# A gated normalisation kernel on one core: the last product of a set's factor moves from DVE to POOL, and a set's chain gets a fourth step

## The chip, the core and the metric

The kernel runs on one core of one Trainium2 chip. The metric is the device time of one execution in microseconds (us). A core has five engines that run side by side, each through its own list of instructions in order: TensorE (PE, matrix products; its weight loads are shown apart as PEld), VectorE (DVE), ScalarE (ACT), GpSimd (POOL) and SyncE (SP, which here only starts loads from memory). They meet through semaphores: an instruction raises one when it is done, and another engine waits until it has reached a count.

## What is computed

x has the shape 8 x 128 x 256 x 256 in float32: 8 batches, 128 channels, 65,536 pixels.

```
def _gn(v, G=32, eps=1e-5):          # per batch, 32 groups of 4 channels
    m, s = mean and variance of a group over its channels and all pixels
    return ((v - m) / sqrt(s + eps))
def _L0_conv_ref(v, W, b):           # v = _gn(x)
    u, var = mean and variance (ddof=1) of v over the 128 channels, per pixel
    n_x = (v - u) / (sqrt(var) + 1e-6)
    n_x = einsum('bchw,oc->bohw', n_x, W) + b
    return v * n_x
out = x + _L0_conv_ref(_gn(x), W, b)
```

So the statistics of a whole batch have to be known before its first pixel can be normalised, and every pixel then needs the reciprocal of its own deviation over the channels. That reciprocal is called the factor.

## The kernel before, in words

**Slots, steps and sets.** A batch is cut in 64 slots of 1,024 pixels (128 partitions by 1,024 columns, 512 KB). One step of the main loop takes one slot through each stage, every stage behind the other by a fixed lag. Four slots make a set, and the small operations on variance and factor are done once for a set, on tiles of 128 by 128. I call a step by its number modulo 4 its phase, 0 to 3.

**What a step does.** POOL normalises the next step's slot in place (L447, `norm`). ACT squares the slot of this step (L575). PE sums slot and squares over the channels (L737), into the set's sums in `sums_ps`. Seven steps behind, PE spreads the factor of a slot to all partitions (L723, into `factor_ps`). Eight steps behind, DVE multiplies the slot by it (L648, `scale`) and PE projects it with W (L749, 16 matrix instructions). Nine steps behind, DVE forms the gated product in place (L662, `gate`), and POOL adds the mean back (L458, `finish`). Ten steps behind, ACT issues the store (L603). PE's order in a step is spread, project, sums. PE's spread waits until DVE's `scale` of the slot before has read `factor_ps`, and DVE's `gate` waits for the projection of its slot.

**A set's chain of small operations.** Counted from the set's first step, it was:

- lag 4, phase 0: ACT squares the channel sums (L594), DVE forms the variance (L668, L672);
- lag 5, phase 1: ACT takes the root, the root plus epsilon and the root squared (L580 to L584), DVE the reciprocal (L680, `approx`), POOL a subtraction and two products that correct it (L491, L465, L467, tile `root`);
- lag 6, phase 2: DVE subtracts 2 from the correction and multiplies by `approx` (L684), which is the factor. Then it is split in three bfloat16 pieces, so that PE can spread it: ACT takes a first piece (L587), POOL the rest (L472), ACT a second piece (L590), POOL the last (L477, `pieces`);
- lag 7, phase 3: PE spreads it.

In ACT's list a pass over a slot of the next batch's statistics stands between the two pieces.

**The next batch's statistics.** While a batch is computed, the 64 slots of the next one are read for mean and variance: 24 by DVE, two `bn_stats` each (L693, L694), at steps of phase 3, two slots at nine of these steps and one at five of them (11, 23, 35, 47 and 55); 40 by ACT, two passes each (L515), in steps 1 to 57. In a step of phase 0, ACT's order is: squares, one pass, the square of the channel sums (L594), the other passes. At steps 58 to 62 the group statistics are worked out by a chain over DVE, ACT and PE.

**Buffers and loads.** x is held in 50 buffers of one slot. 34 slots of the 64 (`KEPT`) stay in their buffer from the statistics to the output; the other 30 are loaded again (`streamed`, L410). The loads for the statistics are L413: item i of 30 to 63 brings the i-30th kept slot. A planner (`Places`) gives each load a planned step: `STATS_LEAD` or `LEAD` steps ahead of its use or earlier, so that two loads are `LOAD_GAP` apart. The plan sets only their order and their buffers. SP goes through that order and issues a load as soon as its buffer is free, which for a kept slot is when that slot's store of the batch before it in the buffer has landed; all later loads wait behind it.

Of the kernel before, what the change touches and what calls it, by code (L numbers as in the profile page):

```python
# [28 lines left out]
KEPT_UNTIL = 42  # L29
# [5 lines left out]
CHAIN_STEPS = 3  # L35

LAG_VAR = SPLIT
LAG_ROOT, LAG_FIT = LAG_VAR + 1, LAG_VAR + 2
# [7 lines left out]
STATS_LEAD = 2  # L46
STORE_STEPS = 2
DROP_STEPS = 2
LOAD_GAP = 0.64
# [140 lines left out]
def norm_gate_kernel(nc, x, w, bias, const, pick, ident, out):  # L190
# [23 lines left out]
    with ExitStack() as ctx:  # L214
# [33 lines left out]
        factor = sum_sq  # L248
# [53 lines left out]
        miss_squared = sem("miss_squared")  # L302
        factor_done = sem("factor_done")
# [128 lines left out]
        def _(pool):  # L432
# [28 lines left out]
            def correct(done):  # L461

                pool.wait_ge(approx_done, done)
                pool.wait_ge(miss_done, done)
                nc.gpsimd.tensor_tensor(miss[:, :], miss[:, :], approx[:, :], ALU.mult).then_inc(miss_scaled, 1)  # L465
                pool.wait_ge(miss_scaled, done)
                nc.gpsimd.tensor_tensor(miss[:, :], miss[:, :], approx[:, :], ALU.mult).then_inc(miss_squared, 1)  # L467

# [11 lines left out]
            def period(b, own, before, nxt):  # L480
                for step in steps(own, before, nxt):
                    root_of = set_behind(step, LAG_ROOT, b, own, before)
# [125 lines left out]
        def _(dve):  # L608
# [28 lines left out]
            def period(b, own, before, nxt):  # L637
                of = plan if own else first_plan
                for step in steps(own, before, nxt):
# [25 lines left out]
                    def var_of_sums(ready):  # L665

                        dve.wait_ge(sum_sq_done, ready)
                        nc.vector.scalar_tensor_tensor(out=var_ps(step - LAG_VAR), in0=sum_sq[:, :], scalar=-1.0 / P,  # L668
                                                       in1=sums_of(step - LAG_VAR)[:, 1, :], op0=ALU.mult, op1=ALU.add)\
                            .then_inc(var_sum_done, 1)  # L670
                        dve.wait_ge(var_sum_done, ready)
                        nc.vector.tensor_scalar(var[:, :], var_ps(step - LAG_VAR), TINY, 1.0 / (P - 1), ALU.max, ALU.mult)\  # L672
                            .then_inc(var_done, 1)
# [4 lines left out]
                    if (ready := set_behind(step, LAG_ROOT, b, own, before)) is not None:  # L678
                        dve.wait_ge(root_eps_done, ready)
                        nc.vector.reciprocal(approx[:, :], approx[:, :]).then_inc(approx_done, 1)  # L680
                    if (ready := set_behind(step, LAG_FIT, b, own, before)) is not None:

                        dve.wait_ge(miss_squared, ready)
                        nc.vector.scalar_tensor_tensor(out=factor[:, :], in0=miss[:, :], scalar=-2.0, in1=approx[:, :],  # L684
                                                       op0=ALU.add, op1=ALU.mult).then_inc(factor_done, 1)
# [110 lines left out]
```

## Time and profile before

| | us |
|---|---|
| time, median of 3 runs | 1874.69 (1874.65 to 1875.2) |
| the profiled execution: its own time | 1875.25 |
| its span from first to last instruction | 1873.4 |
| PE busy | 1695.9 (91%) |
| DVE busy | 1695.0 (90%) |
| ACT busy | 1481.7 (79%) |
| POOL busy | 1455.2 (78%) |

The granted TensorE clock was 0.997 of full speed. 394.49 MB were read and 268.44 MB written, 354 GB/s over the span. Busy time is the union of an engine's instructions; how long an engine waited, and for whom, is in other views, which are shown in the section of rows below.

### The profile page before, as it was taken

How to read it: one execution, taken by the hardware profiler on the slowest of the kernel's cores; microseconds unless marked ns; L12 is line 12 of the kernel's file. 1: busy time of each engine (PE TensorE's matmuls, PEld its weight loads, DVE VectorE, ACT ScalarE, POOL GpSimd, SP SyncE). 2: the span in 40 equal slices, each digit the busy share in tenths (PEclk: the TensorE clock that was granted, in tenths of full speed). 3: DMA queues.
4: the chain of work that ended last, by engine and by line, in shares of the span. 5: the costliest groups of instructions: out<-in, count | busy, mean ns of one | idle time of the engine just before them, and what ended most of it. 6: DMA issues, size and time to landing. Idle time of an engine off the chain costs nothing.

```text
span 1873.4 us, 67650 instructions
## 1 busy us (share of the span) xinstructions
PE 1695.9 (91%) x28706; PEld 918.7 (49%) x28706; DVE 1695.0 (90%) x2000; ACT 1481.7 (79%) x2634; POOL 1455.2 (78%) x1684
## 2 busy tenths in 40 slices
PE   0069999999999999999999999999999999999998
PEld 0045555555555555555555555555555555555553
DVE  5659998999989998999989999999999999888887
ACT  5689887888878887898878889788887988744442
POOL 0058888887888888788788788887887888888885
PEclk9999999999999999999999999999999999999999
DMA  9979999999999999999999999999999999854775
GB/s 375 409 271 370 379 382 329 400 390 397 367 326 413 387 390 349 361 416 378 390 329 395 402 384 379 336 402 389 391 357 356 416 379 398 301 209 188 272 269 216
DMA packets 183037, 667.33 MB, mean 356 GB/s; under 512 B 20560, under 2 KB 20944, under 8 KB 182736
## 3 DMA queue, kind: packets, MB, share of 16 engines
q1 hardware_dynamic: 109008, 394.54, 56.8%
q10 hardware_dynamic: 73728, 268.47, 35.9%
q8 instruction: 227, 3.72, 0.7%
q14 instruction: 74, 0.61, 0.1%
HBM read 394.49 MB, written 268.44 MB: 354 GB/s over the span
## 4 chain that ended last, share of the span: by engine, by line
PE 66%; DVE 15%; issue 6%; DMA 6%; POOL 3%; ACT 2%; SPq 2%; POOLq 0%; ACTq 0%; DVEq 0%
PE proj_ps L749 39%; PE sums_ps L737 15%; PE factor_ps L723 12%; DVE scaled L648 5%; DVE bn L693 4%; DVE bn L694 4%; DMA tiles<-x 4%; SPq L413 2%; DMA out<-tiles 2%; DVE tiles L662 1%; POOL tiles L458 1%; POOL tiles L447 1%; ACT unused L515 1%; ACT squares L575 0%; POOL pieces L477 0%
## 5 line engine op out<-in xcount | busy, mean ns | idle before, releaser
L749 PE MATMUL proj_ps<-scaled,w_t 128*32 128x512 f32 x8192 | 984.9, 598 | 0.1
L458 POOL TENSOR_SCALAR tiles<-tiles,columns_sb 128x1024 f32<-128x1024 f32 x512 | 575.0, 1123 | 231.4 <-DVE tiles L662 227.9
L662 DVE SCALAR_TENSOR_TENSOR tiles<-proj_ps,columns_sb,tiles 128x1024 f32<-128x1024 f32 x512 | 643.6, 1257 | 73.2 <-PE proj_ps L749 71.8
L515 ACT ACTIVATE unused<-tiles,bn 128x1024 uint8<-128x1024 f32 x560 | 635.1, 1134 | 0.0
L648 DVE TENSOR_TENSOR scaled<-tiles,factor_ps 128x1024 f32<-128x1024 f32 x512 | 619.1, 1209 | 10.7 <-PE factor_ps L723 6.5
L447 POOL TENSOR_SCALAR tiles<-tiles,columns_sb 128x1024 f32<-128x1024 f32 x512 | 617.1, 1206 | 13.8 <-DMA tiles<-x 12.8
L575 ACT ACTIVATE squares<-tiles 128x1024 f32<-128x1024 f32 x512 | 537.7, 1050 | 66.1 <-PE sums_ps L737 30.7
L737 PEld LDWEIGHTS sums_ps<-tiles,const_sb 128*32 128x32 f32 x8192 | 245.2, 111 | 317.1 <-issue 263.0
L749 PEld LDWEIGHTS proj_ps<-scaled,w_t 128*32 128x32 f32 x8192 | 213.5, 109 | 360.7 <-issue 306.6
L723 PE MATMUL factor_ps<-pieces,pick_sb 128*128 128x128 bf16 x4096 | 317.7, 220 | 63.3 <-DVE scaled L648 48.4
L737 PE MATMUL sums_ps<-tiles,const_sb 128*32 128x128 f32 x8192 | 319.8, 274 | 13.4 <-ACT squares L575 13.4
L737 PE MATMUL sums_ps<-squares,const_sb 128*32 128x128 f32 x8192 | 319.0, 274 | 0.0
L723 PEld LDWEIGHTS factor_ps<-pieces,pick_sb 128*128 128x128 bf16 x4096 | 231.5, 98 | 172.0 <-issue 76.7
L737 PEld LDWEIGHTS sums_ps<-squares,const_sb 128*32 128x32 f32 x8192 | 235.5, 111 | 0.2
L587 ACT ACTIVATE piece<-sum_sq,const_sb 128x128 bf16<-128x128 f32 x128 | 51.4, 402 | 118.7 <-DVE sum_sq L684 117.5
L680 DVE RECIPROCAL approx<-approx 128x128 f32<-128x128 f32 x128 | 121.3, 948 | 9.9 <-ACT approx L582 7.8
L693 DVE BATCH_NORM_STATS2 bn<-tiles 128x6 f32<-128x512 f32 x168 | 114.4, 681 | 0.0
L694 DVE BATCH_NORM_STATS2 bn<-tiles 128x6 f32<-128x512 f32 x168 | 113.6, 676 | 0.0
L515 ACT ACTIVATION_READ_ACCUMULATOR unused<-tiles,bn 128x1 f32 x560 | 104.9, 187 | 0.0
L760 PE MATMUL sums_ps<-gn,const_sb 128*128 128x1 f32 x16 | 3.2, 271 | 87.7 <-ACT gn L539 87.7
L590 ACT ACTIVATE piece<-sum_sq,const_sb 128x128 bf16<-128x128 f32 x128 | 51.5, 402 | 34.8 <-POOL sum_sq L472 34.8
L441 POOL COPY columns_sb<-new_scalars 128x2 f32<-128x2 f32 x8 | 1.5, 185 | 99.4 <-ACT new_scalars L562 99.4
(58 smaller groups left out, 769.6 us busy)
## 6 DMA issues: line engine op xcount, KB each, us to landing
tiles<-x SPq DMA_DIRECT2D x752, 512.0 KB, 8.5
out<-tiles ACTq DMA_DIRECT2D x512, 512.0 KB, 7.1
const_sb<-const SPq DMA_DIRECT2D x1, 86.0 KB, 1.9
scaled<-w SPq DMA_DIRECT2D x1, 64.0 KB, 2.1
scaled<-ident SPq DMA_DIRECT2D x1, 64.0 KB, 2.0
pick_sb<-pick SPq DMA_DIRECT2D x1, 8.0 KB, 1.8
columns_sb<-bias SPq DMA_DIRECT2D x1, 0.5 KB, 2.4
```

Source lines behind the costliest of these rows:

```text
L447: nc.gpsimd.tensor_scalar(place(s), place(s), norm_scalars[:, 0:1], norm_scalars[:, 1:2], ALU.add, ALU.mult).then_inc(normed, 1)
L458: nc.gpsimd.tensor_scalar(place(s), place(s), 1.0, out_shift[:, 0:1], ALU.mult, ALU.add).then_inc(finished, 1)
L515: nc.scalar.activation(unused[:, which, :], data, (ACT.Identity, ACT.Square)[which], bias=pivot_of(of), scale=-1.0, accum_out=act_sums[:, ...
L575: nc.scalar.activation(squares[:, step % 2, :], place(step), ACT.Square).then_inc(squared, 1)
L648: nc.vector.tensor_tensor(scaled[:, s % 2, :], place(s), factor_ps[:, :], ALU.mult)\
L662: nc.vector.scalar_tensor_tensor(out=place(s), in0=proj_ps[:, s % 2, :], scalar=gate_shift[:, 0:1], in1=place(s), op0=ALU.add, op1=ALU.mul ...
L680: nc.vector.reciprocal(approx[:, :], approx[:, :]).then_inc(approx_done, 1)
L693: nc.vector.bn_stats(bn_of(of)[:, j, :], data[:, 0:BANK])
L694: nc.vector.bn_stats(bn_of(of)[:, j + 1, :], data[:, BANK:SLOT]).then_inc(bn_done, 1)
L723: mm = nc.tensor.matmul(factor_ps[:, chunk(h, t)], pick_sb[:, j:j + 1].to_broadcast([P, P]), pieces[:, s // SPLIT % 2, :], start=True, sto ...
L737: mm = nc.tensor.matmul(sums_of(s)[32 * t:32 * t + 32, which, :], rows, data[:, chunk(h, t)], start=(which == 0 and k == 0), stop=(which = ...
L749: mm = nc.tensor.matmul(proj_ps[q:q + 32, s % 2, h:h + BANK], w_t[:, q:q + 32], scaled[:, s % 2, h:h + BANK], start=True, stop=True)
```

## The change

The product that ends the factor is taken off DVE. POOL does it in two instructions, a shift by -2 and a product, right behind its two correcting products. DVE's reciprocal and POOL's operations move from lag 5 to lag 6 (`LAG_INVERSE`), the pieces from lag 6 to lag 7, and with the longer chain every later stage (spread, scale, gate, store) by one step. The factor is now written into `var` in place of `sum_sq`, so DVE's write of `var` waits for the pieces of the set before. The last kept slot moves from 40 to 42, loads for statistics are planned 1 step ahead of use (it was 2) and at 0.6 steps from each other (it was 0.64). The number of kept slots and so of loads stays.

```diff
-KEPT_UNTIL = 42
+KEPT_UNTIL = 44
...
-CHAIN_STEPS = 3
+CHAIN_STEPS = 4
...
-LAG_ROOT, LAG_FIT = LAG_VAR + 1, LAG_VAR + 2
+LAG_ROOT, LAG_INVERSE, LAG_FIT = LAG_VAR + 1, LAG_VAR + 2, LAG_VAR + 3
...
-STATS_LEAD = 2
+STATS_LEAD = 1
...
-LOAD_GAP = 0.64
+LOAD_GAP = 0.6
...
-        factor = sum_sq
+        factor = var
...
                 nc.gpsimd.tensor_tensor(miss[:, :], miss[:, :], approx[:, :], ALU.mult).then_inc(miss_squared, 1)
+                pool.wait_ge(miss_squared, done)
+                nc.gpsimd.tensor_scalar(miss[:, :], miss[:, :], 1.0, -2.0, ALU.mult, ALU.add).then_inc(miss_shifted, 1)
+                pool.wait_ge(miss_shifted, done)
+                nc.gpsimd.tensor_tensor(factor[:, :], miss[:, :], approx[:, :], ALU.mult).then_inc(factor_done, 1)
...
-                    root_of = set_behind(step, LAG_ROOT, b, own, before)
+                    root_of = set_behind(step, LAG_INVERSE, b, own, before)
...
                         dve.wait_ge(var_sum_done, ready)
+                        if ready > 1:
+                            dve.wait_ge(pieces_done, ready - 1)
...
-                    if (ready := set_behind(step, LAG_ROOT, b, own, before)) is not None:
+                    if (ready := set_behind(step, LAG_INVERSE, b, own, before)) is not None:
                         dve.wait_ge(root_eps_done, ready)
                         nc.vector.reciprocal(approx[:, :], approx[:, :]).then_inc(approx_done, 1)
-                    if (ready := set_behind(step, LAG_FIT, b, own, before)) is not None:
-
-                        dve.wait_ge(miss_squared, ready)
-                        nc.vector.scalar_tensor_tensor(out=factor[:, :], in0=miss[:, :], scalar=-2.0, in1=approx[:, :],
-                                                       op0=ALU.add, op1=ALU.mult).then_inc(factor_done, 1)
```

POOL's list in the middle of a batch, from the `norm` ahead of a set's correcting operations to its last piece. Before:

```order
501 L447 TENSOR_SCALAR tiles<-tiles,columns_sb 128x1024
502 L491 TENSOR_TENSOR root<-var,root 128x128
503 L465 TENSOR_TENSOR root<-root,approx 128x128
504 L467 TENSOR_TENSOR root<-root,approx 128x128
505 L458 TENSOR_SCALAR tiles<-tiles,columns_sb 128x1024
506 L447 TENSOR_SCALAR tiles<-tiles,columns_sb 128x1024
507 L472 TENSOR_TENSOR sum_sq<-sum_sq,piece 128x128
508 L458 TENSOR_SCALAR tiles<-tiles,columns_sb 128x1024
509 L477 TENSOR_TENSOR pieces<-sum_sq,piece 128x128
```

The same stretch in the changed kernel, whose lines are numbered a little higher (L448 is `norm`, L459 `finish`):

```order
562 L448 TENSOR_SCALAR tiles<-tiles,columns_sb 128x1024
563 L496 TENSOR_TENSOR root<-var,root 128x128
564 L466 TENSOR_TENSOR root<-root,approx 128x128
565 L468 TENSOR_TENSOR root<-root,approx 128x128
566 L470 TENSOR_SCALAR root<-root 128x128
567 L472 TENSOR_TENSOR var<-root,approx 128x128
568 L459 TENSOR_SCALAR tiles<-tiles,columns_sb 128x1024
569 L448 TENSOR_SCALAR tiles<-tiles,columns_sb 128x1024
570 L477 TENSOR_TENSOR var<-var,piece 128x128
571 L459 TENSOR_SCALAR tiles<-tiles,columns_sb 128x1024
572 L482 TENSOR_TENSOR pieces<-var,piece 128x128
```

Two instructions have come in ahead of the first `finish`; the rest keeps its order, but the group of five stands in phase 2 now and the pieces in phase 3.

ACT's list at steps 22 to 24 of the first batch, where step 24 is of phase 0 and squares the channel sums of the next set. Before (L587 and L590 are the two pieces, L515 the statistics, L594 the square of the sums):

```order
109 L587 ACTIVATE piece<-sum_sq,const_sb 128x128
110 L515 ACTIVATE unused,act_sums<-tiles,bn 128x1024
111 L590 ACTIVATE piece<-sum_sq,const_sb 128x128
112 L603 DMA out<-tiles 128x1024
113 L575 ACTIVATE squares<-tiles 128x1024
114 L515 ACTIVATE unused,act_sums<-tiles,bn 128x1024 x2
115 L603 DMA out<-tiles 128x1024
116 L575 ACTIVATE squares<-tiles 128x1024
117 L515 ACTIVATE unused,act_sums<-tiles,bn 128x1024
118 L594 ACTIVATE sum_sq<-sums_ps 128x128
```

Steps 23 and 24 in the changed kernel (L592 and L595 are the pieces, L520 the statistics, L599 the square of the sums):

```order
109 L580 ACTIVATE squares<-tiles 128x1024
110 L592 ACTIVATE piece<-var,const_sb 128x128
111 L520 ACTIVATE unused,act_sums<-tiles,bn 128x1024
112 L595 ACTIVATE piece<-var,const_sb 128x128
113 L520 ACTIVATE unused,act_sums<-tiles,bn 128x1024
114 L608 DMA out<-tiles 128x1024
115 L580 ACTIVATE squares<-tiles 128x1024
116 L520 ACTIVATE unused,act_sums<-tiles,bn 128x1024
117 L599 ACTIVATE sum_sq<-sums_ps 128x128
```

Between the second piece and the square of the sums stood a store, a whole step and the beginning of the next (two squares, three passes); now one pass, a store, one squares and one pass stand there.

The third place is the end of SP's list for a batch. It reads alike but for what the buffers' last stores are: items 62 and 63 of the statistics waited for the stores of slots 39 and 40, which ACT issued in steps 49 and 50; now for those of slots 41 and 42, issued in steps 52 and 53. They are used in steps 55 and 56 in both kernels.

## Rows read from the trace of the kernel before

**Rows 1.** The page, busy time of each engine.

```profile
PE 1695.9 (91%) x28706; PEld 918.7 (49%) x28706; DVE 1695.0 (90%) x2000; ACT 1481.7 (79%) x2634; POOL 1455.2 (78%) x1684
```

**Rows 2.** Windows: busy us PE, PEld, DVE, ACT, POOL; clock, DMA share, GB/s.

```profile
580.00:600.00 20.00, 19.24 (x336) 10.56 (x332) 19.26 (x23) 17.21 (x32) 16.81 (x21) 1.00 1.03 416
...
517.00:951.00 434.00, 414.95 (x7044) 224.52 (x7036) 408.86 (x483) 374.51 (x671) 357.96 (x413) 1.00 0.99 379
```

**Rows 3.** Timeline of PE, steps 43 and 44: start, us, instruction, wait.

```profile
904.51 0.62 PE L723 MATMUL factor_ps<-pieces,pick_sb 128*128 128x128 bf16 x8
905.07 1.92 PE L749 MATMUL proj_ps<-scaled,w_t 128*32 128x512 f32 x16
...
908.62 0.62 PE L723 MATMUL factor_ps<-pieces,pick_sb 128*128 128x128 bf16 x8 [0.76 <-DVE scaled L648]
```

**Rows 4.** Timeline of DVE, steps 43 and 44, phases 3 and 0.

```profile
902.16 1.21 DVE L648 TENSOR_TENSOR scaled<-tiles,factor_ps 128x1024 f32<-128x1024 f32 x1
903.78 1.28 DVE L662 SCALAR_TENSOR_TENSOR tiles<-proj_ps,columns_sb,tiles 128x1024 f32<-128x1024 f32 x1 [0.41 <-PE proj_ps L749]
904.98 0.69 DVE L693 BATCH_NORM_STATS2 bn<-tiles 128x6 f32<-128x512 f32 x1
...
907.36 1.21 DVE L648 TENSOR_TENSOR scaled<-tiles,factor_ps 128x1024 f32<-128x1024 f32 x1
```

**Rows 5.** Waits of PE from 517 to 951 us: total, times, longest.

```profile
PE factor_ps L723 <- DVE scaled L648: 13.6, 18, 0.8
PE factor_ps L723 <- POOL pieces L477: 5.2, 4, 1.5
```

**Rows 6.** The removed product: its group, and one at 970 us.

```profile
L684 DVE SCALAR_TENSOR_TENSOR sum_sq<-root,approx 128x128 f32<-128x128 f32 x128 | 57.9, 453 | 2.6 <-POOL root L467 2.6
...
970.74 0.27 DVE L684 SCALAR_TENSOR_TENSOR sum_sq<-root,approx 128x128 f32<-128x128 f32 x1
```

**Rows 7.** Timeline of POOL, steps 45 and 46, phases 1 and 2.

```profile
912.13 0.45 POOL L491 TENSOR_TENSOR root<-var,root 128x128 f32<-128x128 f32 x1
912.72 0.46 POOL L465 TENSOR_TENSOR root<-root,approx 128x128 f32<-128x128 f32 x1
913.26 0.46 POOL L467 TENSOR_TENSOR root<-root,approx 128x128 f32<-128x128 f32 x1
913.71 1.13 POOL L458 TENSOR_SCALAR tiles<-tiles,columns_sb 128x1024 f32<-128x1024 f32 x1
914.82 1.23 POOL L447 TENSOR_SCALAR tiles<-tiles,columns_sb 128x1024 f32<-128x1024 f32 x1
916.01 0.43 POOL L472 TENSOR_TENSOR sum_sq<-sum_sq,piece 128x128 f32<-128x128 f32 x1
```

**Rows 8.** Timeline of ACT, from step 46, and from steps 55 and 56.

```profile
916.48 0.40 ACT L590 ACTIVATE piece<-sum_sq,const_sb 128x128 bf16<-128x128 f32 x1
...
916.93 1.06 ACT L575 ACTIVATE squares<-tiles 128x1024 f32<-128x1024 f32 x1
...
944.95 1.14 ACT L515 ACTIVATE unused<-tiles,bn 128x1024 uint8<-128x1024 f32 x1
...
947.21 1.04 ACT L575 ACTIVATE squares<-tiles 128x1024 f32<-128x1024 f32 x1
948.16 1.14 ACT L515 ACTIVATE unused<-tiles,bn 128x1024 uint8<-128x1024 f32 x1
...
949.30 0.25 ACT L594 ACTIVATE sum_sq<-sums_ps 128x128 f32<-128x128 f32 x1
```

**Rows 9.** Timeline of PE, the spreads of steps 49 and 57.

```profile
925.02 0.62 PE L723 MATMUL factor_ps<-pieces,pick_sb 128*128 128x128 bf16 x8
...
952.09 0.62 PE L723 MATMUL factor_ps<-pieces,pick_sb 128*128 128x128 bf16 x8
```

**Rows 10.** Timeline of DVE, the variance of step 48 and what follows.

```profile
922.43 0.28 DVE L668 SCALAR_TENSOR_TENSOR sums_ps<-sum_sq,sums_ps 128x128 f32<-128x128 f32 x1
...
922.96 1.21 DVE L648 TENSOR_TENSOR scaled<-tiles,factor_ps 128x1024 f32<-128x1024 f32 x1
```

**Rows 11.** Timeline of SP: load issued as slot 42's store lands.

```profile
943.17 0.33 SPq L410 DMA_DIRECT2D tiles<-x  x1
```

**Rows 12.** Loads of L410 issued from 943 to 960 us, six of them.

```profile
DMA to landing us min/median/max: 3.8/5.9/6.6
```

More of the change, by code:

```diff
@@ L302, in norm_gate_kernel @@
         miss_squared = sem("miss_squared")
+        miss_shifted = sem("miss_shifted")
         factor_done = sem("factor_done")
```

## The prediction

> **What bounds the kernel now.** I read the page's busy times first: PE and DVE are both busy for nine tenths of the span, ACT and POOL for under eight [rows 1], so which of the two sets the pace has to come from the timelines. In a stretch of 20 us in the middle of a batch PE is busy for 19.24, and the DMA engines are full too, at 416 GB/s; over two whole batches they move 379 GB/s at a share of 0.99 [rows 2]. The PE timeline gives the unit: the spread of step 43 starts at 904.51. A step of PE without a wait lasts 3.28 us (I read this pitch between nearly all spreads; the spread of step 49 is at 925.02 and that of step 57 at 952.09, eight steps and 27.07 us apart, which is 8 x 3.28 and one further wait of 0.83) [rows 3, 9]. 64 bare steps are 209.9 us. From 904.51 to 908.62, however, PE takes 4.11, and the row names DVE's scale as what it waited for [rows 3]. The reader is to see in the DVE timeline why: scale starts at 902.16 and would be over for the next instruction at 903.3, but gate has to wait for the projection until 903.78; then come gate and four `bn_stats`, and the next scale starts only at 907.36, 1.26 before PE's spread at 908.62 [rows 4, 3]. So the path is PE's projection, gate, 1.20, statistics, 2.38, scale, 1.26. It happens in the nine sets a batch that have two slots of statistics on DVE: 18 waits and 13.6 us in two batches, a little over 0.75 each [rows 5]. The rest of PE's loss lies at the change of batches, where the pieces are late by up to 1.5 us: 5.2 us in two batches [rows 5].
>
> **What it removes.** 128 products on DVE, 57.9 us, 0.45 each [rows 6]. None of it is on the path above. The product stands in phase 2, ahead of phase 3's scale; taking it away makes scale ready earlier, and then gate waits 0.41 plus the 0.45 for the same projection at 903.78 [rows 4]. The cover is PE's own step; if PE's projection came 0.41 sooner than now, the gain would begin. In the sets with one slot or none PE runs at its bare 3.28 already. The reciprocal that moves from phase 1 to phase 2 eats there what the product left, still ahead of 903.78. I count 0, not less.
>
> **What it adds on POOL.** Two instructions a set. Start to start in the chain is 0.59 and 0.54, and 0.45 to the next independent one [rows 7]. A shift of 128 columns isn't in the trace: it costs at least next to nothing beside its hand-over and at most as much as its neighbours, 0.54; I take 0.4, because `finish`, the same operation on eight times the columns, takes 1.13 [rows 7]. The group of five thus lasts about 2.5 where three took 1.58 (912.13 to 913.71), and it stands one step later. What is queued behind it on POOL: finish, the next norm, then the first rest of the pieces, finish, the last piece. I place it in the trace at step 46. With the three gone from phase 1, finish and norm come between 0 and 1.58 earlier; I take 1.0, since finish then waits for gate. Norm starts at 913.8 instead of 914.82, the group at 915.0 (1.19 later), finish at 917.5, norm at 918.6 (1.11), the first rest at 919.8, over at 920.25, finish at 920.2, the last piece at 921.35, over at 921.8. PE's bare spread of step 48 is at 925.02 - 3.28 = 921.74. So the pieces come just in time, 0.1 late in the one-slot sets and hidden behind PE's wait in the others. I count 0.
>
> **What it does to ACT, the first cost.** ACT's second piece waits for that first rest: it starts at 920.3, where it was over a whole step before (916.48 in the row). From there to the variance in phase 0 is now short. Piece to squares 0.45, squares to pass 0.95, pass to the square of the sums 1.14, to the end of it 0.25 [rows 8], hand-over 0.03: the variance starts at 923.1, where it was 922.43. From variance to scale is 0.53 and from scale to the spread 1.26 [rows 10, 4]: 924.9 against 925.02 [rows 9]. It just fits. But where step of phase 3 has two passes of statistics, one of them now lies behind the second piece, as ACT's list shows at step 23: 1.14 more, 926.05, 1.0 late. That is so in steps 23, 35 and 55 of the one-slot sets, and in steps 3, 15 and 43 of the two-slot sets, where 0.8 of it lies beside the wait that is there anyway and 0.2 is left. Without step 55, which follows: 2 x 1.0 + 3 x 0.2 = 2.6 us a batch. Lower end 0 (ACT's second piece comes 1 us earlier than I place it), upper 2 x 2.1 + 3 x 1.3 = 8 (one pass more behind it).
>
> **The loads, the second cost.** Earlier loads have 10 us or more to spare, nearer ones don't matter there; the tail of a batch is tight. Item 62 of the statistics now waits for the store of slot 41 in step 52. In the trace the store that step 52 issues (slot 42) lands at 943.17, when SP issues the load that waited for it [rows 11]. Loads issued there land 3.8 to 6.6 us later, median 5.9 [rows 12]; I take 5, as two such in a row wait on little. So the data is there at 948.2, and ACT's pass over it, the first of step 55, started at 944.95 [rows 8]. What is queued behind it on ACT: the second piece, a pass, squares, a pass, the square of the sums, for which DVE and then PE wait. 948.2 + 1.14 + 0.3 + 1.14 + 0.95 + 1.14 = 952.9, and 0.28 + 0.53 + 1.26 more is 954.9 (rows as above) against the spread at 952.09 [rows 9]: 2.8 us late. Ends: 1.6 with a landing of 3.8, 4.4 with 6.6. Item 63, one step later, is then in time. Later streamed loads wait for the stores of the same steps as before.
>
> **The sum.** One more step of lag costs between nothing and a bare step, 3.28; I take 1.5, as it adds a light step at either end and takes a full one away. At the change of batches the reciprocal and the pieces still stand behind the group statistics; I leave the 2.6 a batch there as it is. Seven batches have a next one: 7 x (2.6 + 2.8) + 1.5 = 39.3. The profiled execution took 1875.25; 1914.6, and as it lies 0.56 above the median of the runs, **1914**.
>
> **Two rules of the skill.** DVE's product took 0.27 at 970.74 and 0.45 in the mean [rows 6]. The Trainium skill, page "SBUF — State Buffer", section "SBUF: two separate sides", says that a DVE operation with two inputs in SBUF and one of GpSimd exclude each other for the whole instruction; the trace agrees with that here, and by it the relief of DVE is the full 57.9 and not 128 x 0.27 = 35, which would raise the faster rival below and changes nothing where gate waits for PE. POOL's product took 0.46 [rows 7] against that 0.27. The Trainium skill, page "GPSIMD Engine Reference", section 3.1 "Elementwise", has GpSimd 1.96 times slower on a product of two tensors, which speaks against this change: an estimate by it is 0.27 x 1.96 = 0.53 for a product, and the chain of five would be some 0.2 longer, the total some 0.2 x 5 x 7 = 7 us more.
>
> **The rivals.**
> - Only one of the two costs comes, 1880 to 1896: chance 0.22. With ACT's alone 7 x 2.6 + 1.5 gives 1894; with the load's alone 1895. For it speaks that each rests on a placing of about 1 us.
> - Neither comes, 1876: chance 0.12. It needs the second piece a microsecond earlier and a landing in under 2 us after the store, or slack on ACT that I don't see. Against it: nothing in rows 12 is under 3.8.
> - Faster: DVE's relief reaches PE, chance 0.14. Place: gate in phase 3 of the two-slot sets. If the projection is in truth not what gate waits for, each of the nine waits of about 0.8 falls by 0.45, 9 x 7 x 0.45 = 28 us, 1847. It decides where gate in phase 3 no longer waits for PE. Against it stands the 0.41 in rows 4.
> - Both costs and more, over 1936: chance 0.05. A late item 58 or 61, which DVE reads just ahead of its scale, passes to PE in full.
> - The forecast, both costs, 1896 to 1936: chance 0.47.
>
> **How the numbers follow.** A measurement of this kernel tells a change from none at about 0.2%, 3.7 us. Slower is the forecast, the single cost and the excess, 0.47 + 0.22 + 0.05 = 0.74; within 0.2% 0.12; faster 0.14. The range from 1874 to 1936 leaves out the faster case and the excess, 0.19. The likeliest case's own range is 1896 to 1936, from the ends of both costs: 7 x (1 + 1.6) at the low one, 7 x (4 + 4.4) at the high one.
>
> **What would show it.** Right if PE's waits for DVE's scale in the sets with two slots stay at about 0.8 although the product is gone, and gate's wait for the projection grows from 0.41; if ACT shows waits for POOL's first rest ahead of the second piece in nearly every set; if new PE waits of about 1 us stand at steps 24 and 36; and if ACT's statistics wait for a DMA at step 55 in each of seven batches, with some 3 us on PE behind it. Wrong if the wait of 0.8 shrinks, if the second piece starts within a microsecond of phase 3's spread, or if the loads of items 62 and 63 land ahead of ACT.

## The result, and the profile after

| | before | changed |
|---|---|---|
| median of 5 runs | 1875.20 us (1874.65 to 1880.19) | 1935.33 us (1934.61 to 1936.22) |
| profiled execution, own time; span | 1875.25; 1873.4 | 1935.33; 1933.5 |

The ratio is 1.0315, 95% interval 1.0304 to 1.0326. The change costs 60 us where 39 were forecast; the 1935.33 lies within the stated range by 0.7 us. The page of the changed kernel, beside [rows 1]:

```profile
PE 1707.7 (88%) x28706; PEld 922.4 (48%) x28706; DVE 1654.6 (86%) x1872; ACT 1471.7 (76%) x2634; POOL 1545.8 (80%) x1940
```

DVE has lost 40 us of work and POOL has gained 91, and the kernel is slower. So the time is in the waits, of the whole execution here (us in total, times, longest):

```profile
ACT piece L595 <- POOL var L477: 167.9, 119, 2.5
DVE sums_ps L673 <- ACT sum_sq L599: 108.9, 70, 10.2
...
DVE tiles L667 <- PE proj_ps L751: 89.9, 163, 0.8
PE factor_ps L725 <- DVE scaled L653: 81.8, 106, 2.0
...
ACT unused L520 <- DMA tiles<-x: 52.8, 29, 4.4
...
PE factor_ps L725 <- POOL pieces L482: 24.4, 23, 3.2
```

Read from below upwards it is a chain: PE waits for scale, DVE for the square of the sums, ACT for POOL's rest of the factor. In the window of PE's waits that answers to [rows 5] (530.50 to 977.20 us, from step 58 to step 56 two batches on) the same stretch takes 446.7 us instead of 434:

```profile
PE factor_ps L725 <- DVE scaled L653: 22.8, 30, 1.3
PE factor_ps L725 <- POOL pieces L482: 6.0, 6, 2.4
```

Eighteen of those waits are the old ones. Steps 43 and 44, PE and then DVE, beside [rows 3, 4]:

```profile
928.66 0.62 PE L725 MATMUL factor_ps<-pieces,pick_sb 128*128 128x128 bf16 x8
...
932.85 0.33 PE L725 MATMUL factor_ps<-pieces,pick_sb 128*128 128x128 bf16 x3 [0.85 <-DVE scaled L653]
```

```profile
926.04 1.22 DVE L653 TENSOR_TENSOR scaled<-tiles,factor_ps 128x1024 f32<-128x1024 f32 x1
927.92 1.28 DVE L667 SCALAR_TENSOR_TENSOR tiles<-proj_ps,columns_sb,tiles 128x1024 f32<-128x1024 f32 x1 [0.66 <-PE proj_ps L751]
929.12 0.69 DVE L695 BATCH_NORM_STATS2 bn<-tiles 128x6 f32<-128x512 f32 x1
...
931.50 1.20 DVE L653 TENSOR_TENSOR scaled<-tiles,factor_ps 128x1024 f32<-128x1024 f32 x1
```

The reader is to see that scale comes earlier, that gate's wait for the projection is 0.66 instead of 0.41, and that PE's wait is 0.85 instead of 0.76: the relief went into gate's wait.

**Where the 60 us are.** I took the distance from the spread of a step to the spread of the next in the PE timeline, less the bare 3.28, and summed it over the profiled execution by the number of the first of the two steps; the wait of 0.85 above counts under step 43. A sum can be under zero because the last eight spreads of the execution are closer together, most of them 2.41 to 3.09 us. The last row is what lies ahead of the first spread and behind the last.

| steps | before | changed | more | forecast |
|---|---|---|---|---|
| the nine with two slots on DVE | 48.5 | 55.3 | 6.7 | 4.2 |
| 24 and 36 | 0.0 | 10.2 | 10.2 | 14.0 |
| 4, 11, 16, 47 and the others in mid-batch | -0.9 | 2.8 | 3.7 | 0 |
| 55 to 59 | 3.8 | 30.0 | 26.2 | 19.6 |
| 60 to 63 and 0 | 14.2 | 25.4 | 11.2 | 0 |
| ahead of the first spread, behind the last | 131.7 | 133.8 | 2.1 | 1.5 |
| sum | | | 60.1 | 39.3 |

In steps 4, 11, 16 and 47 alone the waits come to 6.3 us; the early spreads at the end of the execution take the rest away in that row. The nine cost 0.91 each instead of 0.83. That 0.09 lies between the start of scale and the spread (931.50 to 932.85 against 907.36 to 908.62), and the 0.91 is there in all the kernels with four steps and this placing of the statistics (experiments 3, 4 and 6 to 8), so it goes with the fourth step; what makes it stays open.

**Steps 24 and 36, as forecast.** ACT's timeline at steps 23 and 24, for [rows 8]:

```profile
860.57 0.40 ACT L595 ACTIVATE piece<-var,const_sb 128x128 bf16<-128x128 f32 x1 [1.14 <-POOL var L477]
...
860.88 1.14 ACT L520 ACTIVATE unused<-tiles,bn 128x1024 uint8<-128x1024 f32 x1
...
862.01 1.04 ACT L580 ACTIVATE squares<-tiles 128x1024 f32<-128x1024 f32 x1
...
862.97 1.13 ACT L520 ACTIVATE unused<-tiles,bn 128x1024 uint8<-128x1024 f32 x1
...
864.10 0.25 ACT L599 ACTIVATE sum_sq<-sums_ps 128x128 f32<-128x128 f32 x1
```

And DVE, which waits for the last of these rows ahead of the variance and scale (PE's next spread waits 0.66):

```profile
864.38 0.30 DVE L673 SCALAR_TENSOR_TENSOR sums_ps<-sum_sq,sums_ps 128x128 f32<-128x128 f32 x1 [1.43 <-ACT sum_sq L599]
```

From piece to square of the sums everything is back to back, as the prediction laid it out; each such step costs 0.73 on PE, not 1.0.

**Step 60, not forecast.** ACT in the changed kernel:

```profile
988.45 0.40 ACT L595 ACTIVATE piece<-var,const_sb 128x128 bf16<-128x128 f32 x1 [2.28 <-POOL var L477]
988.76 0.28 ACT L537 ACTIVATE gn<-gn,bn 128x1 f32<-128x1 f32 x1
...
990.94 0.39 ACT L544 ACTIVATE gn<-gn 128x1 f32<-128x1 f32 x1
...
991.80 1.06 ACT L580 ACTIVATE squares<-tiles 128x1024 f32<-128x1024 f32 x1 [0.47 <-ACT gn L544]
992.76 0.26 ACT L599 ACTIVATE sum_sq<-sums_ps 128x128 f32<-128x128 f32 x1
```

The same place before:

```profile
956.99 0.40 ACT L590 ACTIVATE piece<-sum_sq,const_sb 128x128 bf16<-128x128 f32 x1 [1.06 <-POOL sum_sq L472]
...
957.44 1.06 ACT L575 ACTIVATE squares<-tiles 128x1024 f32<-128x1024 f32 x1
958.40 0.28 ACT L532 ACTIVATE gn<-gn,bn 128x1 f32<-128x1 f32 x1
```

Eight small operations of the group statistics (L537 to L544, 2.57 us from the first start to the last end) stand in step 59 of ACT's list. Before, the second piece belonged to step 58, ahead of step 59's squares and of them; now it belongs to step 59 and comes late, they begin only behind it, and the square of the sums comes behind them. DVE waits 2.67 for it and PE 1.6 a batch. It is the mechanism of steps 24 and 36 with eight small operations in place of a pass.

**Step 55.** The pass over item 62, ACT's timeline, and SP's load for it:

```profile
972.94 1.15 ACT L520 ACTIVATE unused<-tiles,bn 128x1024 uint8<-128x1024 f32 x1 [3.31 <-DMA tiles<-x]
...
974.09 0.39 ACT L595 ACTIVATE piece<-var,const_sb 128x128 bf16<-128x128 f32 x1
```

```profile
968.43 0.33 SPq L414 DMA_DIRECT2D tiles<-x  x1
```

The load is issued at 968.43 and the pass can start 4.5 later; 5 was taken from [rows 12]. The delay reaches PE by two ways. The last piece is late behind ACT's second one, and PE waits for it here:

```profile
975.04 0.62 PE L725 MATMUL factor_ps<-pieces,pick_sb 128*128 128x128 bf16 x8 [1.46 <-POOL pieces L482]
```

That makes 2.4 a batch under step 55. The way of the prediction, over the square of the sums and scale, comes after it and makes 1.6 under step 56, 0.7 of which isn't the load's (experiment 3).

**POOL's group of five**, step 58, for [rows 7]:

```profile
983.19 0.47 POOL L496 TENSOR_TENSOR root<-var,root 128x128 f32<-128x128 f32 x1
...
984.89 0.30 POOL L470 TENSOR_SCALAR root<-root 128x128 f32<-128x128 f32 x1
985.27 0.46 POOL L472 TENSOR_TENSOR var<-root,approx 128x128 f32<-128x128 f32 x1
985.72 1.12 POOL L459 TENSOR_SCALAR tiles<-tiles,columns_sb 128x1024 f32<-128x1024 f32 x1
```

It lasts 2.53 (2.5 was forecast); the shift takes 0.38 from its start to the next one's (0.4 was forecast).

### The profile page after: what moved, and what is told of

Its sections match the earlier page's. It is cut to its first block, busy times and chain, and to the rows that moved or that the text cites. A ratio compares the mean times of both kernels' runs of the same rounds, so it can differ in the third digit from the quotient of the medians.

```text
span 1933.5 us, 67905 instructions
## 1 busy us (share of the span) xinstructions
PE 1707.7 (88%) x28706; PEld 922.4 (48%) x28706; DVE 1654.6 (86%) x1872; ACT 1471.7 (76%) x2634; POOL 1545.8 (80%) x1940
## 4 chain that ended last, share of the span: by engine, by line
PE 29%; POOL 22%; DVE 19%; issue 10%; DMA 9%; ACT 8%; SPq 2%; ACTq 1%; POOLq 0%; DVEq 0%
PE proj_ps L751 17%; POOL tiles L459 7%; POOL tiles L448 7%; DVE scaled L653 7%; PE sums_ps L739 6%; PE factor_ps L725 5%; DVE tiles L667 5%; DMA tiles<-x 5%; DMA out<-tiles 4%; ACT unused L520 4%; DVE bn L695 2%; DVE bn L696 2%; SPq L414 2%; POOL root L468 1%; POOL root L466 1%
## 5 line engine op out<-in xcount | busy, mean ns | idle before, releaser
L459 POOL TENSOR_SCALAR tiles<-tiles,columns_sb 128x1024 f32<-128x1024 f32 x512 | 575.1, 1123 | 187.0 <-DVE tiles L667 186.2
L520 ACT ACTIVATE unused<-tiles,bn 128x1024 uint8<-128x1024 f32 x560 | 635.4, 1135 | 27.4 <-DMA tiles<-x 27.3
L653 DVE TENSOR_TENSOR scaled<-tiles,factor_ps 128x1024 f32<-128x1024 f32 x512 | 620.2, 1211 | 10.2 <-PE factor_ps L725 0.7
L448 POOL TENSOR_SCALAR tiles<-tiles,columns_sb 128x1024 f32<-128x1024 f32 x512 | 613.0, 1198 | 9.5 <-DMA tiles<-x 8.7
L595 ACT ACTIVATE piece<-var,const_sb 128x128 bf16<-128x128 f32 x128 | 51.4, 401 | 167.9 <-POOL var L477 167.9
L673 DVE SCALAR_TENSOR_TENSOR sums_ps<-sum_sq,sums_ps 128x128 f32<-128x128 f32 x128 | 37.3, 291 | 109.0 <-ACT sum_sq L599 108.9
L592 ACT ACTIVATE piece<-var,const_sb 128x128 bf16<-128x128 f32 x128 | 51.2, 400 | 90.4 <-POOL var L472 90.2
L520 ACT ACTIVATION_READ_ACCUMULATOR unused<-tiles,bn 128x1 f32 x560 | 104.9, 187 | 0.0
L466 POOL TENSOR_TENSOR root<-root,approx 128x128 f32<-128x128 f32 x128 | 58.7, 458 | 31.0 <-DVE approx L687 12.9
```

The lines of the kernel that those rows point to most:

```text
L448: nc.gpsimd.tensor_scalar(place(s), place(s), norm_scalars[:, 0:1], norm_scalars[:, 1:2], ALU.add, ALU.mult).then_inc(normed, 1)
L459: nc.gpsimd.tensor_scalar(place(s), place(s), 1.0, out_shift[:, 0:1], ALU.mult, ALU.add).then_inc(finished, 1)
L520: nc.scalar.activation(unused[:, which, :], data, (ACT.Identity, ACT.Square)[which], bias=pivot_of(of), scale=-1.0, accum_out=act_sums[:, ...
L653: nc.vector.tensor_tensor(scaled[:, s % 2, :], place(s), factor_ps[:, :], ALU.mult)\
```

## The experiments

My theory was that of the prediction, with step 60 added: the product's removal from DVE is worth nothing, the nine waits of 0.8 are the statistics' and not the chain's, and the loss is ACT's order behind POOL's late rest plus the late last loads. The rival was that the product on DVE is part of those waits, and that the loss is POOL's added work or the fourth step as such. Ratios are against the kernel before, run beside it on the same chip. Spans and sums over steps are those of the one profiled execution of a kernel.

**1. The product on POOL, without the rest** (`pool3`: three chain steps, loads as before).

```diff
 pool.tensor_tensor(miss, miss, approx, mult)
+pool.tensor_scalar(miss, miss, 1.0, -2.0, mult, add)
+pool.tensor_tensor(factor, miss, approx, mult)
...
-dve.scalar_tensor_tensor(factor, miss, -2.0, approx, add, mult)
```

> The kernel before with the product on POOL alone: three chain steps, old lags, old loads. Theory A (the loss comes from where the pieces stand and from the late loads at a batch's tail, and DVE's relief is worth nothing): POOL gets 0.95 us more in phase 1, the last piece, which had 0.5 us to spare ahead of PE's spread in phase 3, comes about 0.45 late; that is hidden in the two-slot sets and costs 5 x 0.45 in the others: 1875 to 1895, no wait of 1 us at steps 24 and 36. Theory B (POOL is overfull with the two operations, wherever they stand): as slow as the changed kernel, 1920 or more. Theory C (relief of DVE is worth something and only the fourth step spoils it): under 1870.

1899.09, ratio 1.0113 (1.0096 to 1.0130), a little above what I expected. By steps, the nine fall from 48.5 to 25.1, but the steps of phase 2 rise from nothing to 41.9: there PE now waits for the pieces, 0.1 to 0.7 a set.

```profile
PE factor_ps L723 <- POOL pieces L482: 54.4, 105, 2.0
...
PE factor_ps L723 <- DVE scaled L653: 23.3, 63, 0.7
```

What falls in the nine is only the half that the lateness one step before has already paid. So a chain of three has no room for the product on POOL; the fourth step is what makes room for it.

**2. The loads alone** (`before_newloads`: `KEPT_UNTIL` 44, `STATS_LEAD` 1, `LOAD_GAP` 0.6 on the kernel before).

> The kernel before with the load plan of the change alone (last kept slot 42, lead 1, gap 0.6). Store to use is 4 steps for the tightest items instead of 6, and 3 in the changed kernel. Theory A: items 62 and 63 land within a microsecond of ACT's use, so the cost is 0 to 1 us a batch, 1875 to 1883. Rival (the nearer plan by itself is what costs, all through the batch): 1895 or more.

1884.77, ratio 1.0043 (1.0023 to 1.0063): slower by itself, a little over what I expected. In its profile steps 55 to 59 cost 16.9 instead of 3.8, all else is within 1 us of before. The profiled execution is one of the two slowest of five (1889.63, where the median is 7.4 above that of the kernel before), so these 13 us are more than the loads cost as a rule.

**3. The change with the last loads' tail as before** (`after_tail6`).

```diff
-KEPT = 34
+KEPT = 33
-KEPT_UNTIL = 44
+KEPT_UNTIL = 41
-STATS_LEAD = 1
+STATS_LEAD = 2
```

> The changed kernel with one kept slot fewer (33), the last kept slot 39 and lead 2, so that store to use is 6 steps again for the tightest items; it loads one slot more a batch. Theory A: the wait of ACT for a DMA at step 55 goes, and with it 2 to 3 of the 4 us that PE loses at steps 55 and 56; steps 24, 36 and 60 to 63 stay: 1910 to 1920. Rival (the late second piece makes all of the loss at step 55, the load lies beside it): 1928 or more.

1916.37, ratio 1.0210 (1.0195 to 1.0226). Steps 55 to 59 fall from 30.0 to 10.0, which is 2.9 a batch for seven batches; the prediction had 2.8. The wait of ACT's pass at step 55 is gone; the 0.7 at step 56 stays.

**4. The product back on DVE, the rest as changed** (`chain4_dve`: four steps, new loads).

```diff
-pool.tensor_scalar(miss, miss, 1.0, -2.0, mult, add)
-pool.tensor_tensor(factor, miss, approx, mult)
...
+dve.scalar_tensor_tensor(factor, miss, -2.0, approx, add, mult)
```

> The changed kernel with the product back on DVE, in phase 3; the fourth step and the new load plan stay. Theory A: POOL's group takes 1.0 us less, the second piece comes that much sooner, the waits at steps 24 and 36 (0.7 each) and the late pieces at 11 and 47 go, DVE's extra product hides in gate's wait; the tail stays: 1912 to 1922. Rival (the fourth step in itself costs, whatever POOL does): 1928 or more. Rival (DVE was relieved with profit): over 1940.

1917.78, ratio 1.0217 (1.0201 to 1.0232). Steps 24 and 36 lose their 10.2, the others in mid-batch 6.6, steps 60 to 0 another 7.8, 5.1 of them at step 63, where PE waited 0.8 a batch for the pieces. The nine rise by 7.1. The product now stands in phase 3 ahead of gate, where it mostly hides in gate's wait (0.91 in six of the nine, as in the changed kernel); in steps 3, 27 and 39, where it takes 1.1 us and not 0.8, each costs 1.2 to 1.35. So the relief of DVE does exist in this order, but it is 7 us where POOL's product costs 24. By the medians, taken one after the other, the 60 us split as follows: the loads 7.4 (1884.77 less 1877.39, with 4 us of doubt either way), the fourth step 33.0 (1917.78 less 1884.77), the product on POOL about 18 (1935.33 less 1917.78).

**5. No product at all** (`no_product`: the kernel before without the subtraction of 2 and the last multiplication; POOL's second correcting product is written as the factor). It leaves out that part of the computation.

> The kernel before without DVE's product (the subtraction of 2 and the last multiplication are left out of the computation; POOL's second product writes the factor's tile instead). DVE is relieved and POOL gets nothing. Theory A (the product hides in gate's wait for the projection): PE's waits of 0.8 in the nine two-slot sets stay as they are, gate's wait for the projection grows; only at step 62, where the pieces hang behind DVE's wait for the group statistics, something can be won, 0 to 1.6 a batch: 1862 to 1878. Rival (DVE's relief reaches PE): the waits of 0.8 fall by up to 0.45, 1850 or less.

1874.95, ratio 0.9994 (0.9984 to 1.0004). This is the cleanest run of the study: 128 products are gone from DVE, nothing is put anywhere, and no time is won. The nine waits sum to 49.0 (48.5 before). PE, and gate in DVE's timeline, at step 43:

```profile
907.57 0.62 PE L718 MATMUL factor_ps<-pieces,pick_sb 128*128 128x128 bf16 x8 [0.76 <-DVE scaled L648]
```

```profile
902.72 1.28 DVE L662 SCALAR_TENSOR_TENSOR tiles<-proj_ps,columns_sb,tiles 128x1024 f32<-128x1024 f32 x1 [0.67 <-PE proj_ps L744]
```

PE's wait is the 0.76 of [rows 3] and gate's has gone from 0.41 to 0.67. That is 0.26 of the 0.49 us that the product ahead of it had held DVE (from its start to that of gate, in the kernel before). Most of the rest is a second cover, which the prediction didn't have: scale can't start before PE has spread its factor. PE's spread, and scale close behind its end:

```profile
900.18 0.62 PE L718 MATMUL factor_ps<-pieces,pick_sb 128*128 128x128 bf16 x8
```

```profile
900.84 1.22 DVE L648 TENSOR_TENSOR scaled<-tiles,factor_ps 128x1024 f32<-128x1024 f32 x1
```

In the kernel before scale started 0.30 behind the end of that spread.

**6 to 8. The three causes taken away.** The square of the sums ahead of the passes (`after_sumfirst`); the eight small operations one step later (`after_gn60`); both, and the loads of experiment 3 (`after_all3`).

```diff
-        SUM_SQ_AFTER = 1
+        SUM_SQ_AFTER = 0
```

```diff
-                    if nxt and step == GN_STEP + 1:
+                    if nxt and step == GN_STEP + 2:
```

> The changed kernel with ACT's pass of statistics of phase 0 behind the square of the channel sums instead of ahead of it; nothing else. Theory A (between the second piece and the square of the sums ACT has a pass too much): PE's waits at steps 24 and 36 (0.7 each), 4 and 16 (0.2) and 0.7 at step 56 go, 2.6 a batch: 1912 to 1922. Rival (the second piece is late for PE by itself): 1930 or more.

1917.46, ratio 1.0228 (1.0210 to 1.0247); the span is 20.8 shorter, in the fastest of its four executions; by the medians it is 18. Steps 24 and 36 have nothing left, nor have 4, 16 and (but for one batch) 47, which were therefore the same cause; 4.3 goes from steps 55 to 59. Step 11 keeps its 0.2 a batch, which only experiment 4 takes away.

> The changed kernel with ACT's eight small operations of the group statistics one step later, at the end of step 60 instead of step 59, so that they don't lie between the second piece and the square of the sums. Theory A: the wait of 1.6 at step 60 goes in each of seven batches, the rest stays: 1920 to 1928. Rival (the group's chain is what counts at the change of batches and gets later): the same microseconds come back at step 61 or 62, 1933 or more.

1926.21, ratio 1.0273 (1.0258 to 1.0288); steps 60 to 0 fall from 25.4 to 16.3, all of it at step 60 (1.6 to 0.2 a batch, as in the kernel before). The span is only 7.3 shorter, since the first spread comes 1.0 later and steps 55 to 59 cost 0.8 more; by the medians it is 9.

> The changed kernel with three things mended: the square of the sums ahead of the pass, the group's small operations one step later, and the loads as in the run with 33 kept slots (six steps from store to use). Theory A, if the terms add: 1916.4 measured with those loads, less 7 x (1.5 + 0.4 + 0.7 + 1.6) = 29: 1882 to 1894, still above the kernel before, because PE's nine waits of 0.8 stay. Rival (something in the longer chain costs that I haven't named): 1900 or more.

1892.00 (1884.63 to 1896.08), ratio 1.0085 (1.0057 to 1.0114). The spans of experiments 6, 7 and 3 are 20.8, 7.3 and 18.7 us under the changed kernel's 1933.5, that of the three together 46.8. By the medians it is 18, 9 and 19 against 43. So the three add up within the noise; that the spans do so to the digit is chance, as the executions of this kernel alone lie up to 11 us apart. In the profiled execution 13 of the 60 us stay: 6.7 in the nine steps, 4.6 in steps 55 to 59 and 1.9 in 60 to 0. By the medians it is 17. No run went after them.

**9. Nothing but the statistics moved** (`spread_bn`, on the kernel before). The function that plans the statistics is given the phases in which DVE may take them. With phase 3 alone two slots fall into nine steps; with phases 2 and 3 each step gets one at most. The loads for these slots are planned a step earlier with them.

```diff
-    plan = plan_statistics(slots, STATS_DVE, STATS_UNTIL, range(3, SPLIT))
+    plan = plan_statistics(slots, STATS_DVE, STATS_UNTIL, range(2, SPLIT))
```

> The kernel before; the only edit is that DVE takes a group's statistics in phases 2 and 3 instead of from phase 3 on, so in a set with two slots on DVE each of the two steps holds one slot's two pairs of bn_stats, not one step both. Theory A (the nine waits of 0.82 a batch are the DVE step with the statistics of two slots: projection, gate, two slots' bn_stats, scale, spread, and no small operation of the chain is in them): the waits at those nine steps shrink or go. DVE's own work in such a set, about 13.5 us by the rows of before against PE's 13.1, then leaves some 0.4 a set: 9 x 0.4 x 7 = 25 of the 52 us remain, median 1840 to 1860, ratio 0.98 to 0.99. Rival B (the waits are the chain's length on DVE, variance to product, wherever the statistics stand): no change within 5 us, 1870 to 1880. Rival C (the statistics one step earlier miss their loads, as the loads are planned for phase 3): above 1880.

1850.23 (1847.15 to 1851.56), ratio 0.9853 (0.9839 to 0.9868): **faster than both kernels**, by 27 us. The nine fall from 48.5 to 3.8, phase 2 rises by 19.0. DVE's timeline at steps 42 and 43:

```profile
884.45 1.21 DVE L648 TENSOR_TENSOR scaled<-tiles,factor_ps 128x1024 f32<-128x1024 f32 x1
885.58 0.33 DVE L684 SCALAR_TENSOR_TENSOR sum_sq<-root,approx 128x128 f32<-128x128 f32 x1
885.84 1.27 DVE L662 SCALAR_TENSOR_TENSOR tiles<-proj_ps,columns_sb,tiles 128x1024 f32<-128x1024 f32 x1
887.03 0.68 DVE L693 BATCH_NORM_STATS2 bn<-tiles 128x6 f32<-128x512 f32 x1
...
888.22 1.20 DVE L648 TENSOR_TENSOR scaled<-tiles,factor_ps 128x1024 f32<-128x1024 f32 x1
...
891.73 1.20 DVE L648 TENSOR_TENSOR scaled<-tiles,factor_ps 128x1024 f32<-128x1024 f32 x1
```

Gate no longer waits; from scale to scale are 3.51 us of DVE's own work, a little over PE's 3.28. DVE is now the bound in these steps, and here the product stands on the path, with 0.26 in step 42 (885.58 to 885.84). That would be 9 x 7 x 0.26 = 16 us if it could go for nothing, an estimate that no run tried.

**10. The same with the product on POOL** (`pool3_spread_bn`: experiments 1 and 9 together).

> The kernel before, with the last product on POOL inside the chain of three steps, and the statistics in phases 2 and 3. With the product alone that chain of three measured 1899, its pieces 0.4 to 0.7 late in every set. Theory A: the 0.3 to 0.4 left at the nine two-slot steps go with the statistics' split and the pieces' lateness of 0.4 to 0.5 one step before stays, so 9 x 0.35 x 7 = 22 us less: 1870 to 1885. Against the run with the split statistics alone it is then 15 to 40 us slower: taking the product from DVE is worth less than its place in the chain costs. Rival: with the product off it DVE is no longer the bound (13.5 less 4 x 0.27 or so is under PE's 13.1), and this one is the faster of the two, below 1850.

1876.44, ratio 1.0000 (0.9991 to 1.0010), 26 us over experiment 9; in experiment 1 the product on POOL cost 22 us (1899.09 against 1877.39) on the old statistics. So in a three-step chain it costs no less where DVE has no room, and the rival (DVE as the bound makes it pay) falls. The nine do lose 5.6 against experiment 9, phase 2 pays 18.1 for it, the others in mid-batch 7.3 and steps 55 to 59 6.6.

**11. Phases 1 and 3** (`before_bn13`, the same line with `(1, 3)`).

> The kernel before, with DVE's statistics in phases 1 and 3. Theory A as for phases 2 and 3: each DVE step holds at most one slot's statistics, so most of the 52 us go; but phase 1 also holds the reciprocal, so 1840 to 1865. Rival B (chain length): 1870 to 1880. Rival C: the statistics two steps earlier wait for loads that are planned for phase 3, above 1880, and the wait of PE is then at the steps before 55 to 60 too.

1881.72, ratio 1.0023 (1.0013 to 1.0032). None of the three cases. The nine have nothing left (-1.3), but steps of phase 1 now wait 0.4 to 1.5 each, 54 us. DVE's timeline at steps 20 and 21:

```profile
827.95 1.21 DVE L648 TENSOR_TENSOR scaled<-tiles,factor_ps 128x1024 f32<-128x1024 f32 x1
830.13 0.95 DVE L680 RECIPROCAL approx<-approx 128x128 f32<-128x128 f32 x1 [0.97 <-ACT approx L582]
831.00 1.18 DVE L662 SCALAR_TENSOR_TENSOR tiles<-proj_ps,columns_sb,tiles 128x1024 f32<-128x1024 f32 x1
832.10 0.68 DVE L693 BATCH_NORM_STATS2 bn<-tiles 128x6 f32<-128x512 f32 x1
...
833.30 1.20 DVE L648 TENSOR_TENSOR scaled<-tiles,factor_ps 128x1024 f32<-128x1024 f32 x1
```

One reciprocal with its wait for ACT, 1.84 from 829.16 to 831.00, takes the room of the second slot's statistics; 5.35 from scale to scale. I had seen that phase 1 holds the reciprocal and priced it far too low.

**12. The repaired change with phases 1 and 3** (`after_all13`: experiment 8 with `(1, 3)`; in the chain of four the reciprocal stands in phase 2).

> The changed kernel with the three repairs (sum of squares first, moments one step later, last loads as before; 1892 measured) and DVE's statistics in phases 1 and 3. Theory A: its nine waits of 0.87 to 0.9 a batch are again the step with two slots' statistics; with DVE free of the product its work in such a set, about 12.4 us, is under PE's 13.1, so all nine can go: 9 x 0.87 x 7 = 55 less, 1837 to 1862. Then the product on POOL is worth something, and only once the statistics no longer stand in one step. Rival: the planned loads (0.6 steps apart and nearer to their use) come too late for statistics in phase 1: no gain, above 1885.

1875.37, ratio 0.9992 (0.9976 to 1.0007), 17 us under experiment 8 where 30 to 55 were expected. The nine fall from 55.3 to 15.8, 39 us of the 55 that I looked for, and steps 55 to 59 rise from 8.4 to 27.8. POOL's timeline at step 55 shows what is late there, the load of a streamed slot for `norm`, and behind it the rest of the factor:

```profile
938.35 1.20 POOL L448 TENSOR_SCALAR tiles<-tiles,columns_sb 128x1024 f32<-128x1024 f32 x1 [1.75 <-DMA tiles<-x]
939.50 0.43 POOL L477 TENSOR_TENSOR var<-var,piece 128x128 f32<-128x128 f32 x1
```

PE's spread then waits 1.83 for the pieces. Whether the buffers' order or the full DMA engines make that load late stays open: no run changed it.

## Why the prediction was right, and where its size was off

- **DVE's relief counted as 0: right.** Shown by experiment 5 at 0.9994. Gate's wait took up what scale won, but only 0.26 of it, to 0.67, where 0.45 more were forecast; the rest lies in scale's own wait for the spread. In the order with four steps the relief is 7 us (experiment 4), since there the product would stand in phase 3.
- **POOL's group of five 2.5, pieces just in time: right.** 2.53; in mid-batch PE waits for the pieces at steps 11 and 47 alone in the changed kernel, 0.2 to 0.6, and in most sets in experiment 1, where they have one step less.
- **ACT's second piece, the first cost: right in mechanism and place, and incomplete.** Steps 24 and 36 were to cost 2 x 1.0 a batch and cost 2 x 0.73. The piece starts 1.67 after phase 3's spread (860.57 against 858.90), where 1.84 was placed (920.3 against 918.46); the other 0.1 is a shorter way from there to the spread. But the same lateness also reaches steps 4, 16 and 47 with 0.2 to 0.6, and step 56 with the 0.7 that stays in experiment 3, which "Without step 55, which follows" left out. Experiment 6 took 20.8 us away in all, against the 18.2 of this term: the sum was near, its places were not.
- **The late load, the second cost: right in size, in part by another way.** 2.8 a batch forecast, 2.9 measured by experiment 3. The prediction led it over the square of the sums to scale; most of it reaches PE a step earlier, over the late last piece. Without the fourth step (experiment 2) it is 1.9 in the profile and 1.1 by the median; there the stores come a step earlier, which I take to be the reason.
- **The step that failed is "At the change of batches the reciprocal and the pieces still stand behind the group statistics; I leave the 2.6 a batch there as it is."** By my sum over the steps it was 2.0 a batch and rose to 3.6 (14.2 and 25.4 over seven batches). 1.4 more come at step 60: ACT's eight small operations stand behind the late second piece, shown by experiment 7. 0.9 more come at step 63, where PE waits 0.8 for the pieces: in the changed kernel's timeline DVE's reciprocal of the set stands behind a wait of 2.20 for the group statistics, and POOL's group of five comes behind that. With the product back on DVE (experiment 4) 0.7 of it go. Some 0.6 less at steps 62 and 0 no run took apart. I had followed the second piece through ACT's list up to where a pass stood behind it, and not on to step 59, where eight small operations do.
- **One step more of lag, +1.5:** 2.1.

The terms that were missed or short are thus 11.2 (change of batches), 6.6 (step 56 for the most part), 3.7 (mid-batch), 2.5 (the nine steps) and 0.6 (the lag); 3.8 (steps 24 and 36) was too much: 39.3 + 20.8 = 60.1.

That 1935 still lies in the range is luck. What came is both costs and 21 us that the sum didn't have, in kind the rival "Both costs and more", which had a chance of 0.05 and another place. The range's upper end, 1936, came from the two costs alone and took 4 us a batch for the first, where the paragraph on it gives 0 to 8; with 8 it would be about 1963, and with 0 at the low end about 1886.

## What to carry to other kernels

Before taking work off an engine that is 90% busy, look at what ends its waits in the steps that are slow: if it waits there for the engine it feeds, the relief goes into that wait, and a kernel with the work simply left out tells it in one run. Count what falls together in one step rather than over the span: the same statistics, at most one slot a step instead of two, won 27 us, and put beside a reciprocal that waits they lost them again. When an operation becomes late, walk down the whole list of the engine behind it for one full batch, the rare steps too: each place with anything between it and the next operation that others wait for has a price.

## What the hardware showed unasked

DVE's product of 128 by 128 depends on what POOL does beside it. Its mean was 0.453 us in the kernel before, with single ones from 0.27 to 1.16, and in experiment 4 0.765:

```profile
L687 DVE SCALAR_TENSOR_TENSOR var<-root,approx 128x128 f32<-128x128 f32 x128 | 97.9, 765 | 1.8 <-POOL root L468 1.8
```

In both kernels 120 of the 128 start while POOL's `finish` runs. How much of `finish` is left decides. In experiment 4, POOL and DVE:

```profile
893.19 1.12 POOL L459 TENSOR_SCALAR tiles<-tiles,columns_sb 128x1024 f32<-128x1024 f32 x1
893.69 0.76 DVE L687 SCALAR_TENSOR_TENSOR var<-root,approx 128x128 f32<-128x128 f32 x1
```

The product ends 0.14 us behind `finish`. Of the 128, 114 in the kernel before and 124 in experiment 4 end 0.13 to 0.16 behind the POOL instruction that ran when they started: the product lasts as long as that one has left, and 0.14 more. The seven that met an idle POOL in the kernel before took 0.27, and so nearly (0.29) did those that started within 0.05 of POOL's instruction. In experiment 4 the product started earlier in `finish`, typically 0.50 behind its start instead of 0.71, and so it took longer. This is the exclusion of the two engines that the prediction named, and the trace bears it out.

So with 0.46 for a product on POOL the two engines were on a par here. The Trainium skill, page "GPSIMD Engine Reference", section 3.1 "Elementwise", has POOL 1.96 times slower on an add of two tensors. Against the products that ran alone (0.27) POOL's was 1.7 times slower here. I had expected neither the par nor that the same instruction would get slower by being moved one step.
